# Four-tile groups instead of two-tile pairs in the prefix-state pass of a linear-attention and mixture-of-experts layer

## The reference, cut to what matters

```python
x = x + _L0_attn_ref(_layernorm(x), Wqkv, bqkv, Wout, bout, slopes)
x = x + _L0_ffn_ref(_layernorm(x), w_gate, wi_0, wi_1, wo)

# lightning_attn, per block of 64 tokens, S carried over the whole sequence
scores = einsum('bhid,bhjd->bhij', qb, kb) * intra_decay
o      = einsum('bhij,bhjd->bhid', scores, vb) + einsum('bhid,bhde->bhie', qb * q_decay, S)
S_new  = blk_decay * S + einsum('bhjd,bhje->bhde', kb * k_decay, vb)
```

## Time and profile before

| | us |
|---|---|
| median of the two runs shown | 7164.41 |
| the two runs | 7050.45 and 7278.37 |
| the profiled execution | 7022.79 |
| its span (slowest core, core 7) | 7021.7 |
| spans of its eight cores | 6987.8 to 7021.7 |

### The profile page before, as it was taken

How to read it: one execution, slowest core, us unless ns; L and a number is a source line. 1 busy time by engine, 2 the same in 40 slices (tenths; PEclk the granted TensorE clock), 3 DMA queues, 4 the chain that set the end, 5 groups by cost and what they waited for, 6 DMA issues and landing times.

```text
span 7021.7 us, 41101 instructions; the slowest of 8 cores (6987.8 to 7021.7 us)
## 1 busy us (share of the span) xinstructions
PE 3140.5 (45%) x13620; PEld 1339.0 (19%) x13620; DVE 916.8 (13%) x1673; ACT 932.0 (13%) x2604; POOL 0.2 (0%) x4
## 2 busy tenths in 40 slices
PE   0004422412413314224120577334445888888888
PEld 0001110101101101001010233112112333333333
DVE  1110011010010010110101100133111111111111
ACT  1001111201111111112011210044211000000000
POOL 0000000000000000000000000000000000000000
PEclk9998655656656656556565688655677999999999
DMA  6763335344344343353444111300234111211112
GB/s 203 260 210 118 143 138 182 117 144 175 119 149 169 122 176 141 141 182 117 143 149 168 54 66 54 132 25 1 85 125 162 60 60 63 70 66 60 60 61 78
DMA packets 231546, 833.50 MB, mean 119 GB/s; under 512 B 13936, under 2 KB 14193, under 8 KB 192428
## 3 DMA queue, kind: packets, MB, share of 16 engines
q10 hardware_dynamic: 78336, 444.63, 18.3%
q1 hardware_dynamic: 153008, 386.24, 15.1%
HBM read 679.81 MB, written 151.01 MB: 118 GB/s over the span
## 4 chain that ended last, share of the span: by engine, by line
PE 42%; DMA 30%; ACT 10%; DVE 9%; issue 7%; ACTq 1%; SPq 1%; DVEq 0%
DMA s_cvf<-wffn_im 16%; DMA s_wcg<-wqkvb 7%; PE pb L407 6%; PE pb L409 5%; PE pb L939 4%; DMA s_wqcf<-wqkv 3%; PE pb L941 3%; DVE s_cvb L298 3%; PE pb L895 3%; PE pb L898 3%; PE pb L896 3%; PE pb L897 3%; PE pb L523 3%; PE pb L525 3%; PE pb L340 2%
## 5 line engine op out<-in xcount | busy, mean ns | idle before, releaser
L340 PE MATMUL pb<-s_ident,s_lntile 128*128 128x128 bf16 x512 | 135.7, 265 | 2098.8 <-ACT s_lntile L330 1855.7
L407 PE MATMUL pb<-s_wcg,s_lnT 128*128 128x512 bf16 x1536 | 651.3, 424 | 499.8 <-DMA s_wcg<-wqkvb 490.0
L409 PE MATMUL pb<-s_wcg,s_lnT 128*128 128x512 bf16 x1536 | 647.6, 422 | 0.0
L939 PE MATMUL pb<-s_wo,s_inter 128*128 128x512 bf16 x1024 | 397.1, 388 | 238.5 <-DVE s_out L954 208.9
L340 PEld LDWEIGHTS pb<-s_ident,s_lntile 128*128 128x128 bf16 x512 | 53.7, 105 | 2182.0 <-issue 2182.0
L895 PE MATMUL pb<-s_lnT,s_wi 128*128 128x512 bf16 x1024 | 389.0, 380 | 29.4 <-DMA s_wi<-wall 17.3
L941 PE MATMUL pb<-s_wo,s_inter 128*128 128x512 bf16 x1024 | 397.0, 388 | 0.0
L298 DVE CAST s_cvb<-s_cvf 128x2048 bf16<-128x2048 f32 x192 | 235.6, 1227 | 1234.8 <-DMA s_cvf<-wffn_im 1234.8
L896 PE MATMUL pb<-s_lnT,s_wi 128*128 128x512 bf16 x1024 | 388.9, 380 | 0.0
L898 PE MATMUL pb<-s_lnT,s_wi 128*128 128x512 bf16 x1024 | 388.9, 380 | 0.0
L897 PE MATMUL pb<-s_lnT,s_wi 128*128 128x512 bf16 x1024 | 388.9, 380 | 0.0
(11 more groups left out here) (118 smaller groups left out, 2943.4 us busy)
## 6 DMA issues: line engine op xcount, KB each, us to landing
s_wcg<-wqkvb SPq DMA_DIRECT2D x108, 2048.0 KB, 12.1
s_cvf<-wffn_im ACTq DMA_DIRECT2D x192, 1024.0 KB, 5.8
wall<-s_cvb ACTq DMA_DIRECT2D x192, 512.0 KB, 2.9
s_wi<-wall ACTq DMA_DIRECT2D x128, 512.0 KB, 4.3
s_wqcf<-wqkv ACTq DMA_DIRECT2D x16, 3072.0 KB, 14.8
s_wostr<-woutb SPq DMA_DIRECT2D x64, 512.0 KB, 3.3
s_wo<-wall SPq DMA_DIRECT2D x16, 2048.0 KB, 8.3
s_xstr<-xp SPq DMA_DIRECT2D x24, 1024.0 KB, 14.2
```

What stands on the lines that cost most here:

```text
L340: t.inc(ten.transpose(pbankb(bk, P), s_lntile[:, par * C + ch * P: par * C + (ch + 1) * P], s_ident[:]), pe)
L407: ten.matmul(pbank(2 * j, 512), lhs, s_wcg[:, i * KB:i * KB + 512], start=st_, stop=False)
L409: ten.matmul(pbank(2 * j + 1, 512), lhs, s_wcg[:, i * KB + 512:(i + 1) * KB], start=st_, stop=False)
L939: ten.matmul(pbank(ybanks[0], 512), lhs, wosl[:, hc * KB: hc * KB + 512], start=st_, stop=sp)
```

## The change

The prefix pass is written anew. Nothing outside it changes.

- 24 tiles are handled in 6 groups `g` of four tiles, with no 13th turn. Each column group is loaded once for four tiles, and PE does 128 matmuls and eight bias matmuls for it, in all eight PSUM banks. ACT then copies eight banks to `s_kvst`, which now holds one group of four tiles instead of two pairs.
- The state update of a group follows its own column groups in the same turn: for each head one decay activation of four columns, four scaled K tiles (in `s_kbd`, `s_qbd`, `s_qT`, `s_qdT`), four matmuls accumulating in bank 4 or 5, and one add.
- The transposes use PSUM banks 0 and 1 (before: 4 and 5).
- `emit_ffn_conv(28)` is emitted between the transposes and the first column group of a turn, and `emit_ffn_conv(2)` at the end of a turn. With the 24 at the start, the last turn's first call has 18 strips left and its second none.

The core of the diff:

```diff
-    for p in range(NPP + 1):
-        if p < NPP:
-            for j in range(2):
-                pt = 2 * p + j
-                ... (x load, emit_ln_tile)
-                emit_transposes(par, (p % 2) * 2 + j, banks=(4, 5))
-            e_lnT_av = t.count[av]
-            for cg in range(4):
-                ... (s_bout and s_wcg loads)
-                t.wait(ten, av, e_lnT_av)
-                for i in range(NCH):
-                    for j in range(2):
-                        ... (two matmuls)
-                t.wait(scal, pe, kv_mm_ev[p])
-                for j in range(2):
-                    ... (two copies to s_kvst)
-        if p >= 1:
-            pm = p - 1
-            for h in range(H):
-                ... (s_rs, two scaled tiles, two matmuls, one add)
-            emit_ffn_conv(14)
+    for g in range(6):
+        for pt4 in range(4):
+            pt = g * 4 + pt4
+            par = pt % 2
+            if pt >= 2:
+                t.wait(sync, av, ln_state["apply"].get(pt - 2, 0))
+                t.wait(sync, dv, ln_state["stats_dv"].get(pt - 2, 0))
+            t.inc(sync.dma_start(out=s_xstr[:, par * C:(par + 1) * C],
+                                 in_=d_xp[pt * P:(pt + 1) * P, :]), dXp[par], 16)
+            ...
+            pfx_lnT_pe, _ = emit_transposes(par, pt4)
+        emit_ffn_conv(28)
+        for cg in range(4):
+            ... (s_bout and s_wcg loads, as before)
+            t.wait(ten, av, t.count[av])
+            if e_prev_kv_mm:
+                t.wait(ten, av, kv_evac_ev)
+            if e_prev_u_dv:
+                t.wait(ten, dv, e_prev_u_dv)
+            for i in range(NCH):
+                for pt4 in range(4):
+                    ... (two matmuls)
+            t.wait(scal, pe, e_prev_kv_mm)
+            for pt4 in range(4):
+                ... (two copies to s_kvst)
+            kv_evac_ev = t.count[av]
+        t.wait(ten, av, kv_evac_ev)
+        for h in range(H):
+            ... (s_rs, four scaled tiles, four matmuls, one add)
+        e_prev_u_dv = t.count[dv]
+        e_prefix_pe = t.count[pe]
+        emit_ffn_conv(2)
```

More of the change, by code:

```diff
@@ L349, in build_program @@
     e_s0_ms = t.count[dv]
-    NPP = 12
-    wcg_user = {0: 0}
+    wcg_user = {}
     wcg_ld = {}
     ub_dv = {}
+    e_prev_u_dv = 0
+    brow_ld = 0
+    x_ev = {}
+    pfx_lnT_pe = 0
     pfx_u_mm = {}
[L355 to L359, removed]
-    for p in range(NPP + 1):
-        if p < NPP:
-            for j in range(2):
-                pt = 2 * p + j
[L364 to L377, removed]
-                emit_transposes(par, (p % 2) * 2 + j, banks=(4, 5))
-            e_lnT_av = t.count[av]
-            for cg in range(4):
[L381 to L397, removed]
-                t.wait(ten, av, e_lnT_av)
[L399 to L402, removed]
-                for i in range(NCH):
-                    for j in range(2):
[L405 to L411, removed]
-                for j in range(2):
[L413 to L419, removed]
-                t.wait(scal, pe, kv_mm_ev[p])
[L421 to L427, removed]
-        if p >= 1:
-            pm = p - 1
-            t.wait(ten, av, kv_evac_ev[(pm, 3)])
-            for h in range(H):
[L432 to L460, removed]
-            emit_ffn_conv(14)
@@ new lines, in build_program @@
+    e_prev_kv_mm = 0
+    e_prefix_pe = 0
+    sbf_gate = 0
+    for g in range(6):
[7 more added lines that the diff above has]
+                                 in_=d_xp[pt * P:(pt + 1) * P, :]), dXp[par], 16)
+            x_ev[pt] = t.count[dXp[par]]
+            t.wait(vec, dXp[par], x_ev[pt])
+            if pt == 0:
+                t.wait(vec, dv, e_s0_ms)
+            sd, ap = emit_ln_tile(s_xstr[:, par * C:(par + 1) * C], par,
+                                  pfx_lnT_pe if pt >= 2 else 0)
+            ln_state["stats_dv"][pt] = sd
+            ln_state["apply"][pt] = ap
+            pfx_lnT_pe, _ = emit_transposes(par, pt4)
+        emit_ffn_conv(28)
+        for cg in range(4):
+            colbase = C + cg * KB
+            t.wait(sync, dB, e_bias_st)
+            if brow_ld:
+                t.wait(sync, pe, brow_pe_gate)
+            t.inc(sync.dma_start(out=s_bout[0:1, 0:KB], in_=d_biasb[0:1, colbase:colbase + KB]), dR, 16)
+            brow_ld = t.count[dR]
+            for hf in range(2):
+                if (g, cg) != (0, 0):
+                    t.wait(sync, pe, wcg_user.get(0, 0))
+                elif hf == 0:
+                    t.wait(sync, dQs[0], wq_st[NCH - 2])
+                    t.wait(sync, dQs[1], wq_st[NCH - 1])
+                src = d_wqkvb[hf * KB:(hf + 1) * KB, colbase:colbase + KB].rearrange(
+                    "(c p) n -> p c n", p=P)
+                dst = s_wcg[:, hf * 8 * KB:(hf + 1) * 8 * KB].rearrange("p (c n) -> p c n", n=KB)
+                t.inc(sync.dma_start(out=dst, in_=src), dWp[hf], 16)
+                wcg_ld[hf] = t.count[dWp[hf]]
+            t.wait(ten, av, t.count[av])
[3 more added lines that the diff above has]
+                t.wait(ten, dv, e_prev_u_dv)
+            t.wait(ten, dWp[0], wcg_ld[0])
+            t.wait(ten, dWp[1], wcg_ld[1])
+            for i in range(NCH):
+                for pt4 in range(4):
+                    lhs = s_lnT[:, i * KB + pt4 * P: i * KB + (pt4 + 1) * P]
+                    st_ = (i == 0)
+                    ten.matmul(pbank(2 * pt4, 512), lhs, s_wcg[:, i * KB:i * KB + 512],
+                               start=st_, stop=False)
+                    ten.matmul(pbank(2 * pt4 + 1, 512), lhs, s_wcg[:, i * KB + 512:(i + 1) * KB],
+                               start=st_, stop=False)
+            t.wait(ten, dR, brow_ld)
+            for pt4 in range(4):
+                ten.matmul(pbank(2 * pt4, 512), s_onesb[:], s_bout[0:1, 0:512],
+                           start=False, stop=True)
+                mm = ten.matmul(pbank(2 * pt4 + 1, 512), s_onesb[:], s_bout[0:1, 512:KB],
+                                start=False, stop=True)
+            e_prev_kv_mm = t.inc(mm, pe)
+            brow_pe_gate = e_prev_kv_mm
+            wcg_user[0] = e_prev_kv_mm
+            t.wait(scal, pe, e_prev_kv_mm)
+            if g == 0 and cg == 0:
+                t.wait(scal, dv, e_wg)
+            for pt4 in range(4):
+                base = pt4 * 4096 + cg * KB
+                t.inc(scal.copy(s_kvst[:, base:base + 512], pbank(2 * pt4, 512)), av)
+                t.inc(scal.copy(s_kvst[:, base + 512:base + KB], pbank(2 * pt4 + 1, 512)), av)
+            kv_evac_ev = t.count[av]
+        t.wait(ten, av, kv_evac_ev)
+        for h in range(H):
+            par2 = h % 2
+            t.wait(scal, av, t.count[av])
+            t.inc(scal.activation(s_rs[:, 0:4], s_ptsc[:, g * 4:(g + 1) * 4], AF.Exp,
+                                  scale=s_negs[:, h:h + 1]), av)
+            t.wait(scal, av, t.count[av])
+            if pfx_u_mm.get(par2):
+                t.wait(scal, pe, pfx_u_mm[par2])
+            for pt4 in range(4):
+                dstsl = (s_kbd, s_qbd, s_qT, s_qdT)[pt4][:, par2 * P:(par2 + 1) * P]
+                t.inc(scal.activation(dstsl,
+                                      s_kvst[:, pt4 * 4096 + h * P: pt4 * 4096 + (h + 1) * P],
+                                      AF.Identity, scale=s_rs[:, pt4:pt4 + 1]), av)
+            e_ksc = t.count[av]
+            t.wait(ten, av, e_ksc)
+            if par2 in ub_dv:
+                t.wait(ten, dv, ub_dv[par2])
+            for pt4 in range(4):
+                srcsl = (s_kbd, s_qbd, s_qT, s_qdT)[pt4][:, par2 * P:(par2 + 1) * P]
+                mm = ten.matmul(pbank(4 + par2, P), srcsl,
+                                s_kvst[:, pt4 * 4096 + 2048 + h * P: pt4 * 4096 + 2048 + (h + 1) * P],
+                                start=(pt4 == 0), stop=(pt4 == 3))
+            pfx_u_mm[par2] = t.inc(mm, pe)
+            t.wait(vec, pe, pfx_u_mm[par2])
+            t.wait(vec, dv, t.count[dv])
+            t.inc(vec.tensor_tensor(s_S0[:, h * P:(h + 1) * P], s_S0[:, h * P:(h + 1) * P],
+                                    pbank(4 + par2, P), ALU.add), dv)
+            ub_dv[par2] = t.count[dv]
+        e_prev_u_dv = t.count[dv]
+        e_prefix_pe = t.count[pe]
+        emit_ffn_conv(2)
@@ L462, in build_program @@
     e_S0 = t.count[dv]
-    e_prefix_pe = t.count[pe]
     e_prefix_av = t.count[av]
-    e_prev_u_dv = t.count[dv]
     ln_state["tp"] = ln_state["tp"]
```

## The result

The changed kernel took 6715.11 us (median of 11 runs, 6441.69 to 6859.34) against 7059.13 us (median of 10, 7015.8 to 7292.48). The ratio is 0.9162, with a 95% interval of 0.9113 to 0.921.

The account below looks back on a forecast made before the run. The prefix pass was taken as a row of stages where one thing runs and the rest waits. Five turns of 469.8 us and a sixth of 376.9 made 2725.9, saving 594: 6429, given as 6455 us, range 6370 to 6600.

Parts of the forecast that it names:

- The turn's sum: One turn of the new prefix pass: stage times added to 459.8 us without contention, 469.8 with 10 for the collision.
- conversions with the collision: The 28 conversions behind a turn's transposes: 216.7 us at 7.74 each, plus 10 for weights landing among them.
- copies and restart: ACT's eight copies of column group 0 behind the 28 conversions, then PE starting again: 4.4 us a turn.
- column groups: Column groups 1 to 3 of a turn, twice 45.7 us and 31.8 for the last block: 123.2 us.
- the rest: End of a turn: two conversions at 15.5 us, then 3.2 to the next table load.
- The collision: Column group 1's weights landing amid conversions, six times: 10 us each taken, between nothing and 13.0.
- The other reading of the collision: With a 358 GB/s core share, weights fit beside the conversions at no cost, 60 us less; the prediction rejected it.
- the old collision: At the start, 4 MB of weights stretched three conversion loads by 13.0 us; its going away was to give 13 back.
- The late tile: Third and fourth tile's loads waiting on layer norm: 0 taken in the sum, up to 85 us if shown in full.
- Group 0's block was covered: Rival: PE starts column group 0 only after the 28 conversions, 211 us more in all, 6640 us; chance 4%.
- the rival's 13/16: Rival: PE's 18 uncovered blocks run at 13/16 of the rate, 7.3 us longer each, 132 in all, 6561; chance 4%.
- Conversions were not stretched throughout: Rival: every conversion load in the pass takes 11.5 us instead of 5.8, 958 us added, 7330 us; chance 2%.

## Why the prediction was right

- **Where the kernel was bound.** Right: the experiments put weights gaps, PE blocks and conversions on the path, each near the price read from the earlier trace rows.
- **The turn's sum.** Term by term, predicted and measured in the second turn: layer norm and transposes 63.2 and 62.8; conversions with the collision 226.7 and 226.7; copies and restart 4.4 and 4.6; column groups 123.2 and 122.8; copies 4.1 and 4.1; state update 29.5 and 29.4; the rest 18.7 and 17.2. The pass came out 17.5 us shorter than predicted, mostly from two later turns of 461.0 and 463.8 us; full turns scatter by that much (460.8 to 482.1 us on cores 0, 3, 4 and 7), and why is open.
- **The collision.** 10 was taken, between bounds of 0 and 13.0, and 10.8 was measured. That it came so close is partly luck, since the case that it was read from the earlier trace rows holds less. The changed kernel issues its first weights only at 549.39, and its first three conversion loads are still 7.8 us over 5.8 in all:

```profile
331.01 10.25 DMA s_cvf<-wffn_im
...
343.01 7.85 DMA s_cvf<-wffn_im
...
352.67 7.09 DMA s_cvf<-wffn_im
```

  So of the 13.0 us, 5.2 were the weights (4.3 to 8.7 on the eight cores); the rest has another cause, of which the prediction named one, the end of a store. Why the same 4 MB cost 10.8 us in the pass is open; the weights of another core, seen above, are a candidate. Two or three longer loads had been forecast, and there were five.
- **The other reading of the collision.** The HBM Reference of the Trainium skill (Specifications) gives a core a share of about 358 GB/s, and no run here contradicts that. The reading put on it, that the weights fit into what the conversions leave of the share, was wrong. While the weights landed, from 1096.9 to 1113.8, the DMA engines were at 0.99 and moved 344 GB/s, although over the whole call the share was only 0.61: for those 17 us there was nothing left beside the weights, and the conversion loads among them were stretched.
- **The start.** 13 us had been claimed back from the old collision. This step was wrong: by the rows above some 5 us went. The pass began 9.3 us earlier on core 7, but between 14.4 us earlier and 6.7 us later on the eight cores, so the claim can't be read from the start times. In the total it is outweighed by the pass, which was 17.5 us shorter than its sum.
- **Covered at nothing.** The late tile cost nothing: the second turn's four applies of layer norm are 15.4 us apart throughout.
- **Rivals.** Group 0's block was covered, shown by 136 PE instructions in the window of conversions. The blocks were not slower: 31.9, 31.6 and 32.4 us for the uncovered ones of the second turn, where the own stage of before has 31.8 and 32.3. Each starts at a granted clock of 0.50, the lower level, and is at 1.00 for its last 24 to 27 us; the rival's 13/16 shows in none of them. Conversions were not stretched throughout: the median landing on core 7 is 5.9 us.
- **The absolute number.** 6455 was given and the least times of the changed kernel were 6441.7 and 6449.6. As a ratio, 6429 / 7022.8 = 0.915 was predicted and 0.916 measured. The median of all 11 runs, 6715, lies above the range of 6370 to 6600: the prediction allowed only 2% for causes outside the change, and the longest of these runs is 6.5% above the shortest.

What the prediction missed is no term of the sum but a question: whether the conversions had to be exposed at all. It priced them at 1300 us before and after alike and left it there.

## What to carry to other kernels

A wait for a DMA emitted on a compute engine's queue is a stretch of free cover: count what else can run inside it, and spread it over all blocks that need cover instead of giving it to one. Then look at which transfers start at the same moment; a wait that sets their order can be worth more than the work that it delays. When two gains cover the same gaps, measure each alone: they need not add.

## What the runs showed of the hardware

- Conversions with one load of 1 MB under way at a time moved 199 GB/s, loads and stores together, in a cycle of 7.74 us; with two under way, 302 GB/s in 5.64 us, a weights load among them.
- What a collision costs, and whom, went with the number of loads under way. A 4 MB load beside a stream with one 1 MB load under way cost the stream 10.8 us and landed in 16.4 us itself. Issued into a stream with two under way, it took 34.7 us instead of 12.3. While it landed in the first case, the DMA share was 0.99 at 344 GB/s.
- Conversion loads of 7.0 to 8.0 us appeared on the four odd-numbered cores before their own weights were issued, and were gone when all cores held their weights back.
- A DMA issue emitted behind eight ACT copies went out 0.23 us after the first of them began, 3.8 us before the last one ended.
